# A two-layer decoder on one core: keys and values made further ahead, in room taken from three buffers, with a new hand-written order

## The reference

```python
# layer 0
x = x + self_attn(norm(x))            # 16 heads of 8, causal, softmax
x = x + cross_attn(norm(x), ctx) + bo # 8 heads of 64, keys and values from ctx
x = x + ternary_ffn(norm(x))          # one 128x128 product of quantised values
# layer 1
x = x + self_attn(norm(x))            # scores clipped to +-10, causal
x = x + cross_attn(norm(x), ctx)      # 16 heads of 64
x = x + moe(norm(x))                  # 8 experts of 128x128, gate by softmax,
                                      # gates under 0.1 dropped, rest renormalised
```

## Time and profile before

| | |
|---|---|
| median of 3 runs | 517.37 us (516.3 to 519.82) |
| the profiled execution | 516.53 us, of which the span of the profile is 514.5 us |
| TensorE busy | 491.8 us (96%) |
| TensorE weight loads | 417.4 us (81%) |
| ScalarE busy | 440.0 us (86%) |
| VectorE busy | 409.7 us (80%) |
| POOL busy | 393.6 us (77%) |
| mean granted TensorE clock | 0.991 |

### The profile page before, as it was taken

The page is one execution under the profiler, slowest core; times in us unless marked ns, Lnnn a source line. Parts: engine busy times, 40 slices in busy tenths (PEclk is TensorE's granted clock), DMA queues, the critical chain, the costliest instruction groups (busy, mean ns, idle before and its releaser), DMA issues.

```text
span 514.5 us, 15998 instructions
## 1 busy us (share of the span) xinstructions
PE 491.8 (96%) x5499; PEld 417.4 (81%) x5499; DVE 409.7 (80%) x937; ACT 440.0 (86%) x1177; POOL 393.6 (77%) x557
## 2 busy tenths in 40 slices
PE   7999999999999999999999999999999999989983
PEld 3887886878998888788898888888988888777772
DVE  4868778986898898988888898887888787877663
ACT  5888888999898888998899898999799898798741
POOL 4687588885888788868889776887787787775664
PEclk9999999999999999999999999999999999999996
DMA  6900000000000000000000000000000000000000
GB/s 194 341 5 1 1 3 2 2 2 3 1 2 7 3 8 2 2 6 9 2 1 8 3 5 5 1 6 4 2 11 3 3 2 8 6 2 7 6 6 11
DMA packets 6462, 8.95 MB, mean 17 GB/s; under 512 B 1008, under 2 KB 4848, under 8 KB 6384
## 3 DMA queue, kind: packets, MB, share of 16 engines
q1 hardware_dynamic: 6384, 7.94, 4.7%
HBM read 6.50 MB, written 1.05 MB: 15 GB/s over the span
## 4 chain that ended last, share of the span: by engine, by line
PE 77%; ACT 7%; issue 4%; DVE 4%; POOLq 3%; POOL 3%; DVEq 1%; DMA 0%; ACTq 0%
PE psum L1171 12%; PE psum L1158 9%; PE psum L1198 8%; PE psum L1226 8%; PE psum L1115 8%; PE psum L1145 5%; PE psum L1184 3%; PE psum L1331 2%; PE psum L1237 2%; ACT diff_cross L770 2%; PE psum L1217 2%; PE psum L1186 2%; PE psum L1218 2%; PE psum L1219 2%; PE psum L1209 2%
## 5 line engine op out<-in xcount | busy, mean ns | idle before, releaser
L690 POOL TENSOR_TENSOR w_low_self<-w_self 128x1024 f16<-128x1024 f32 x64 | 120.7, 1894 | 13.9 <-ACT w_self L753 8.6
L770 ACT ACTIVATE diff_cross<-psum,row_max_cross 128x128 f32<-128x128 f32 x384 | 104.5, 410 | 7.9 <-DVE row_max_cross L913 7.4
L695 POOL TENSOR_TENSOR diff_cross<-diff_cross,e_rec_cross 128x1024 f32<-128x1024 f32 x48 | 90.8, 1897 | 14.8 <-DVE e_rec_cross L922 13.9
L913 DVE TENSOR_REDUCE row_max_cross<-psum 128x8 f32<-128x1024 f32 x48 | 58.0, 1218 | 17.8 <-PE psum L1158 17.7
L920 DVE TENSOR_REDUCE e_sum_cross<-diff_cross 128x8 f32<-128x1024 f32 x48 | 58.3, 1215 | 2.0 <-ACT diff_cross L770 1.9
L780 ACT ACTIVATE w_cross<-psum 128x1024 f32<-128x1024 f32 x48 | 49.9, 1049 | 6.0 <-PE psum L1171 5.1
L1158 PE MATMUL psum<-kT_cross,qT_cross 64*128 64x128 f32 x768 | 53.2, 282 | 0.5 <-ACT qT_cross L735 0.3
L1198 PEld LDWEIGHTS psum<-w_cross,v_cross 128*64 128x64 f32 x768 | 41.1, 136 | 15.4 <-issue 13.7
L1198 PE MATMUL psum<-w_cross,v_cross 128*64 128x128 f32 x768 | 51.3, 278 | 0.3 <-issue 0.2
L1158 PEld LDWEIGHTS psum<-kT_cross,qT_cross 64*128 64x128 f32 x768 | 46.0, 187 | 6.4 <-issue 4.2
L1171 PE MATMUL psum<-ident,diff_cross 128*128 128x128 f32 x384 | 49.3, 273 | 0.4 <-ACT by_head_self L735 0.3
(11 more groups left out here) (194 smaller groups left out, 1398.4 us busy)
## 6 DMA issues: line engine op xcount, KB each, us to landing
out_dram<-x_all SPq DMA_DIRECT2D x16, 64.0 KB, 1.5
x_all<-in_x SPq DMA_DIRECT2D x1, 768.0 KB, 7.4
cT_all<-in_ctx SPq DMA_DIRECT2D x1, 768.0 KB, 9.2
e_k<-in_e_k SPq DMA_DIRECT2D x1, 512.0 KB, 4.9
e_v<-in_e_v SPq DMA_DIRECT2D x1, 512.0 KB, 5.8
e_q<-in_e_q SPq DMA_DIRECT2D x1, 512.0 KB, 8.9
e_o<-in_e_o SPq DMA_DIRECT2D x1, 512.0 KB, 9.8
m_w<-in_m_w SPq DMA_DIRECT2D x1, 512.0 KB, 8.7
```

The costliest lines, as they stand in the source:

```text
L690: pool.tensor_tensor(L.w_low[u][:], L.w[u][:], halves(L.w[u][:]), ALU.subtract)\
L695: pool.tensor_tensor(L.diff[u][:].rearrange("p (h k) -> p h k", h=UNIT), L.e[u][:].rearrange("p (h k) -> p h k", h=UNIT), L.e_rec[:, u, :] ...
L770: last = act.activation(L.e[u][:, P * p:P * (p + 1)], S_[:, P * p:P * (p + 1)], ACT.Exp, bias=L.row_max[:, u, p:p + 1])
L913: dve.tensor_reduce(L.row_max[:, u, :], group(i, turn)[:].rearrange("p (h k) -> p h k", h=UNIT), AX_X, ALU.max, negate=True).then_inc(L.ma ...
```

## The change

It does six things.

1. `AHEAD` goes from 6 and 4 to 8 and 6 sequences.
2. The room for that comes from: the cross-attention's `diff` becomes the same buffer as `w` (three buffers less), so the exponentials of a sequence wait until the product with the values of the sequence before is done; `w_low` becomes the unused low 16 bits of each word of `w`, written and read at a step of 4 bytes; the masks are stored once and read four times over by a broadcast operand; `ones` and `mix` move into `weighted`.
3. `weighted` now also holds `mix`, so `ml` of a sequence waits for `o` of the one before.
4. For the last sequence the sum over the experts and the sum with `x` are made by VectorE, not by POOL.
5. `keep_busy` puts 4, 2 and 3 multiplications without use before `xT`, `g` and `e` of the last sequence, into banks that these overwrite.
6. The orders of TensorE, ScalarE, VectorE and POOL are new. The steps are the same ones.

```diff
-AHEAD = dict(cross0=6, cross1=4)
+AHEAD = dict(cross0=8, cross1=6)
...
-            add(f"{L}.ex.{c}", "ACT", 2060, [f"{L}.mx.{c}"], [f"{L}.t.{c}"], half=1030)
+            add(f"{L}.ex.{c}", "ACT", 2060, [f"{L}.mx.{c}"], [f"{L}.pv.{c}"], half=1030)
...
-            self.diff = self.w if width == SD else [sb(f"diff{u}", [P, UN]) for u in range(units)]
+            self.diff = self.w
...
-        self.w_low = [self.sb(f"w_low{u}", [P, UN], FP16) for u in range(2)]
+        self.w_low = [w[:].bitcast(FP16).rearrange("p (n two) -> p n two", two=2)[:, :, 0] for w in self.w]
...
-        mask = [sb(f"mask{j}", [P, 4, P], BF16) for j in range(4)]
+        mask = [sb(f"mask{j}", [P, P], BF16) for j in range(4)]
...
-        mix = sb("mix", [P, P])
+        mix = weighted[:, 1, :]
...
             def mix_experts(i):
+                if i == NSEQ - 1:
+                    return
...
                 act.wait_ge(L.max_ready[u], i + 1)
                 if i:
-                    act.wait_ge(s_full, score(i - 1, f"{L.name}.t.{u}"))
+                    act.wait_ge(x_full, full(i - 1, f"{L.name}.pv.{u}"))
...
                 if i:
-                    dve.wait_ge(mixed, i)
+                    dve.wait_ge(*emptied(i - 1, "moe.b"))
...
             def finish(i):
+                if i == NSEQ - 1:
+                    dve.drain()
+                    dve.tensor_reduce(moe.xn[:], weighted[:].rearrange("p e d -> p d e"), AX_X, ALU.add)
+                    dve.drain()
+                    dve.tensor_tensor(mix, moe.xn[:], x_all[:, i, :], ALU.add)
+                    dve.drain()
+                else:
+                    dve.wait_ge(mixed, i + 1)
                 dve.wait_ge(x_full, full(i, "moe.b"))
-                dve.wait_ge(mixed, i + 1)
...
-                                  ident_b[rows, rows], mask[j][rows, :, :].rearrange("p h k -> p (h k)"),
+                                  ident_b[rows, rows], mask[j][rows, :].unsqueeze(1).broadcast_to([32, 4, P]),
...
+            def keep_busy(place, n):
+
+                for _ in range(n):
+                    pe.matmul(place.rearrange("p (h k) -> p h k", h=4), ident_b[:],
+                              mask[0][:].unsqueeze(1).broadcast_to([P, 4, P]), start=True, stop=True)
...
                 if step == "xT":
+                    room(i, name)
+                    if L is moe and i == NSEQ - 1:
+                        keep_busy(bank(i, name), 4)
                     pe.wait_ge(units_ready if L is ffn else L.xn_ready, i + 1)
```

More of the change, by code:

```diff
@@ L168, in all_steps @@
     add("moe.gTe", "ACT", 167, ["moe.gT"])
-    add("moe.ml", "DVE", 1150, ["moe.e", "moe.w"])
+    add("moe.ml", "DVE", 1150, ["moe.e", "moe.w"], ["moe.o"])
     add("moe.sm", "POOL", 3293, ["moe.ml"], ["moe.o"])
@@ new lines @@
+        "aWb4aSbMbAbPbIbicgbsa8b4cpa3aFbIbPbMaNbAbsaDaFb4cgaScpaWbAcwbibPbMbIa8aNcJcwcpcgb4bsaSaWaFbIbMbPbicJ"
+        "bAa8cwcga3b4cpaNbsaSaFaWbIcJbibMbPa8bAcwcpcga3a3aNaSbsb4aWaFbMbPbIcJbia8aFbAcwcpb4cgbsaNaSaWcJbMbIbi"
+        "bPa8bAaNcwa3cgcpaFb4bsaWaScJbPbibIa3bMa3a8bAcwcgb4aFbIaNbsaScpaWbibPbMcJbAcwa8cpa3aNbscgb4aSaWcJbMbi"
+        "bPa8cwbIbAaNcga3cpaWaSbsb4cJaNbiaSa8a3aWbIbAcwcgcpbMa8bPbsbib4cJbPa3bIcwbibMbsbAcgcpb4cJbsbIbMbPbAcw"
+        "cgcpb4bIbAcJbMbPcwcgbIb4cpbMbPb4cpcgcwcJcgcpcwcJcwcJcJ"
@@ L496, in decoder @@
         x_bias = [sb(f"x_bias{b}", [P, P]) for b in range(2)]
-        ones = sb("ones", [P, P])
         t_abs = sb("t_abs", [P, 1])
@@ L552, in decoder @@
         weighted = sb("weighted", [P, EXPERTS, P])
-        mix = sb("mix", [P, P])
-        t_unit, t_round = weighted[:, 0, :], weighted[:, 1, :]
+        mix = weighted[:, 1, :]
+        t_unit, t_round, ones = weighted[:, 0, :], weighted[:, 1, :], weighted[:, 2, :]
         bias_added = sem("bias_added")
@@ L632, in _ @@
                     for j in range(1, 4):
-                        sp.dma_start(mask[j][32 * j:P, :, :], mask[0][0:P - 32 * j, :, :]).then_inc(masks_turned, 16)
-                        sp.dma_start(mask[j][0:32 * j, :, :], mask[0][P - 32 * j:P, :, :]).then_inc(masks_turned, 16)
+                        sp.dma_start(mask[j][32 * j:P, :], mask[0][0:P - 32 * j, :]).then_inc(masks_turned, 16)
+                        sp.dma_start(mask[j][0:32 * j, :], mask[0][P - 32 * j:P, :]).then_inc(masks_turned, 16)
             for i in range(NSEQ):
@@ L689, in low @@
                     pool.wait_ge(*taken(i, f"{L.name}.s1", u))
-                pool.tensor_tensor(L.w_low[u][:], L.w[u][:], halves(L.w[u][:]), ALU.subtract)\
+                pool.tensor_tensor(L.w_low[u], L.w[u][:], halves(L.w[u][:]), ALU.subtract)\
                     .then_inc(L.low_ready[u], 1)
@@ L709, in mix_experts @@
                 pool.drain()
[L710 removed]
+                pool.tensor_tensor(mix, weighted[:, 0, :], x_all[:, i, :], ALU.add).then_inc(mixed, 1)
             def do_step(i, name, L, step, u):
@@ L776, in weights_by_key @@
                 turn = f"{L.name}.t.{u}"
-                if i:
-                    act.wait_ge(x_full, full(i - 1, f"{L.name}.pv.{u}"))
                 act.wait_ge(s_full, score(i, turn))
@@ L1013, in finish @@
             def finish(i):
+                if i == NSEQ - 1:
[6 more added lines that the diff above has]
+                    dve.wait_ge(mixed, i + 1)
                 dve.wait_ge(x_full, full(i, "moe.b"))
-                dve.wait_ge(mixed, i + 1)
-                dve.tensor_tensor(x_all[:, i, :], bank(i, "moe.b")[:, 0:P], mix[:], ALU.add)\
+                dve.tensor_tensor(x_all[:, i, :], bank(i, "moe.b")[:, 0:P], mix, ALU.add)\
                     .then_inc(emptied(i, "moe.b")[0], 1)
@@ L1092, in _ @@
             dve.memset(shift[:], SHIFT)
-            dve.memset(ones[:], 1.0)
+            dve.memset(ones, 1.0)
             dve.memset(g_weight[:], 0.0).then_inc(consts, 1)
@@ L1129, in self_scores1 @@
                         rows = slice(32 * r, 32 * (r + 1))
-                        pe.matmul(group(i, name, j // 2)[queries, 512 * (j % 2):512 * (j % 2 + 1)],
-                                  ident_b[rows, rows], mask[j][rows, :, :].rearrange("p h k -> p (h k)"),
+                        pe.matmul(group(i, name, j // 2)[queries, 512 * (j % 2):512 * (j % 2 + 1)]
+                                  .rearrange("p (h k) -> p h k", h=4),
+                                  ident_b[rows, rows], mask[j][rows, :].unsqueeze(1).broadcast_to([32, 4, P]),
                                   start=True, stop=False)
@@ L1299, in moe_step @@
                         pe.wait_ge(loaded["moe"], load_count("moe"))
+                    room(i, name)
+                    if i == NSEQ - 1:
+                        keep_busy(bank(i, name), 2)
                     pe.wait_ge(moe_high, i + 1)
-                    room(i, name)
                     pe.matmul(bank(i, name)[:, 0:EXPERTS], moe_xnT[:], wt["m_g"][:], start=True, stop=True)\
@@ L1306, in moe_step @@
                         pe.wait_ge(lo_ready["m_w"], 1)
+                    room(i, name)
+                    if i == NSEQ - 1:
+                        keep_busy(group(i, name)[:, 0:512], 3)
                     pe.wait_ge(*emptied(i, "moe.xT"))
-                    room(i, name)
                     for half in range(2):
@@ L1336, in do_step @@
                     room(i, name)
-                    pe.matmul(bank(i, name)[:, 0:1], ones[:], t_abs[:], start=True, stop=True).then_inc(x_full, 1)
+                    pe.matmul(bank(i, name)[:, 0:1], ones, t_abs[:], start=True, stop=True).then_inc(x_full, 1)
                 elif L in (self0, self1):
```

90 lines of the change are left out of this document (42 added, 48 removed).

## The result

The changed kernel takes 510.61 us (median of four runs, 509.18 to 512.14) against 516.85 us for the kernel before on the same chip (516.3 to 519.82): ratio 0.9867 with an interval of 0.984 to 0.9894, so 1.3% faster (the ratio is of means; the two medians alone give 0.988). The forecast was 512.0 us. The profiled execution spans 507.1 us, against 514.5.

The account below looks back on a forecast made before the run. TensorE, saturated from 130 to 430 us, was taken as the bound, with idle only at the edges. From 516.53 us, 6.8 saved and 2.2 lost give 511.9, stated as 512.0; forecast range 509.5 to 514, chance 0.47.

Parts of the forecast that it names:

- Bound: From 130 to 430 us TensorE idles 0.6 us in 300 and is the bound; added TensorE work costs full price.
- Late fillers: Eight key and value steps moved behind `cross1.y[11]` fill TensorE's waits: 3.6 us saved, bounds 0 and 4.1.
- the two fillers of the last sequence: From 480 us on: cover 1.0 us before `cross1.y[14]` but delay `cross1.t.0[15]`; 0.4 us charged.
- Early fill: Two more key and value steps before `cross1.y[0]` take back 1.0 us of 3.0 idle from 40 to 130 us.
- The tail: Last sequence: `ml` starts 0.4 us earlier, VectorE's sum saves 1.75 us; together 2.2 us, bounds 0.7 and 2.6.
- The start: First scores move ahead of three key steps and wait for masks until some 9.5 us; costs 0.7 us, bounds 0 to 1.3.
- The fallen clock: Rival, chance 0.08: TensorE's longer idle at the start drops its clock; some 4 us of work at half rate, 514 us.
- Changes of shape: Eight more changes of TensorE's array shape, almost all in saturated time, cost 0.14 us each, 1.1 us.
- Buffers: Low halves at a step of 4 bytes and broadcast masks have no price on POOL or TensorE: 0 us.
- the rival with POOL's in-place halves: Rival, chance 0.07: in-place 16-bit writes are dearer on POOL; slower from about 1.4 us more each, 550 us at twice the price.
- The exponentials' wait: ScalarE's new wait for the previous sequence's `pv` is hidden: ahead of the scores in 32 of 45 cases.
- full gain: Rival, chance 0.18: remaining early and late idle vanishes and short gaps in the saturated stretch tighten by 2 us; 507.5 us.

Follow-up runs that it names:

- the run without them: Changed kernel with eight of its eleven key and value steps behind `cross1.y[11]` moved ahead of it: 516.72 us, 0.9988 to the kernel before.
- three swaps: Changed kernel with three late value steps each put behind the step whose wait it covered: 513.13 us in a single run, span 511.1.
- extra products: Changed kernel plus one unused product before each of 64 output projections: with 64 rows (changes array shape) 526.54 us, with 128 rows (control) 515.91 us.
- late scores in this order: Changed kernel with TensorE's first eight and ScalarE's first twelve steps ordered as in the kernel before: 515.49 us, 0.9961 to the kernel before.
- the same two lines: Cross-attention's `diff` placed in `w`, exponentials waiting for `pv`; run with shared halves and masks in the kernel before, old orders and `AHEAD`: 527.99 us, 1.0202.

## Why the prediction was right, point by point

The time lies 1.4 us under the forecast and inside its own range, 509.5 to 514. Several terms were off, in both directions.

**Bound.** Right. The 300 saturated microseconds stayed saturated, and each step put there cost its full time and more (0.80 us for 0.70).

**Late fillers: right in mechanism, too small.** The sum had 3.6 - 0.4 = 3.2 us; idle time gives 4.6, the run without them 5.8. The 3.6 us from 430 to 480 us were near: idle there went from 4.1 us to 0.95. The step that was mis-sized is the 0.4 us charged for the two fillers of the last sequence: in that last stretch (480 to 500 us before, 475 to 494 after) idle went from 2.1 us to 0.63, the 1.0 us before `cross1.y[14]` went and nothing took its place. And a named wait is not all that a cover saves: three swaps cost 2.6 us for 1.8 us of such waits.

**Early fill: right**, 1.5 us by the idle time, 1.0 expected. The two more fillers that stand ahead of `y[0]` are in it.

**The tail: 1.45 us, not 2.2.** (The 1.7 us behind `y[15]` hold 0.3 us more of the store, whose time from the last sum to the end of the span is 1.9 to 2.3 us among these profiles.) The term that was mis-sized is the reduction. It was costed at 1.22 us by L920, which reads neighbours; here the next element to be summed lies 512 bytes further, and 128 sums of 8 are made instead of 8 sums of 128; it took 1.87 us. Which of the two makes the difference, no run sets apart. The start of `ml` was right: 0.35 us earlier relative to the residual sum, 0.4 expected, because the gate weights (500.87) decide now and not the experts (500.27). But the 0.14 us that the dummies bring shows that the clock was little of that.

**The start: the size about right, for another reason.** The sum charged 0.7 us because TensorE would idle longer and "everything that follows is saturated". In the first profile neither shows: idle is 3.6 us against 3.7, the scores began at 9.18 us, 0.3 us sooner than the 9.5 expected, and `cross1.y[0]` is 2.1 us early, 1.5 of it the early fill. But that is the fastest execution. The seven profiles without extra products start `y[0]` at 130.4 to 133.0 us, 132.0 in the middle, against 132.5 before; less the 1.5 us of the early fill, which all but one of them show (idle from 40 to 130 us 1.4 to 1.5 us, in that one 2.0), the start runs from a gain of 0.5 us to a loss of 2.0, with a loss of 1.0 in the middle. That the charge of 0.7 comes near is luck, since the loss is the fallen clock or VectorE behind POOL. And what follows is not TensorE's bound until the first sequence's chain has run: with late scores in this order TensorE waits 4.3 us for VectorE from 13 to 40 us. The prediction looked only at who is idle now, not at what gets late.
The Trainium skill, DMA: Bandwidth & Descriptors (the table at its head), says a transfer under 512 bytes is read, modified and written. The trace doesn't bear out a price here: the last mask copy, with rows of 256 bytes, landed in 1.8 us, with rows of 1024 bytes in 2.2. That is one copy each, and the small one also moves a quarter of the bytes.

**The fallen clock: a rival with too low a chance.** It had 0.08 and came in four of nine profiles of this start, at 1.5 to 2.6 us, about the 2 us forecast. Together with the wait for VectorE it spreads the kernel's times (509.2 to 512.1) rather than decides the verdict.

**Changes of shape: right in kind.** 0.14 us expected, 0.11 measured: 0.9 us for eight, not 1.1. The 0.14 was the difference between two single units and a pair, which can as well be read as the price of two changes, 0.07 each; the measured 0.07 to 0.11 leave both open. TensorEngine Tiling (Array Packing) of the Trainium skill, Key Properties, says that a change drains TensorE, and the trace agrees with these 0.11 us.

**Buffers.** Halves and masks cost nothing (0.9999), as argued from the earlier trace rows; the rival with POOL's in-place halves is out. The exponentials' wait was called hidden; that holds only for the new order. In the old one the same two lines cost 2%. So the new orders avoid a loss of 10 us that no view of the kernel before could show, since the wait didn't exist there.

**The sum by what was measured:** 5.8 (late) + 1.5 (early) + 1.45 (tail) + 0.2 (start) - 0.9 (shape) = 8.05 us, against 7.4 between the profiled spans; with 4.6 for the late fillers it is 6.85. So 7.4 lies between the two readings. It is also the gain of the fastest execution; between the medians it is 6.2 us. The prediction's own sum was 4.6 us. The "full gain" of 507.5 us was not met (510.6 the median; 509.18, the fastest, lies just inside its range). Its reason, shorter gaps inside busy time in the saturated stretch, is not borne out: from `y[0]` to `y[11]` the new order has 6.0 us less of steps by the planner's figures, and takes 4.4 us less.

**What no run separates:** whether `AHEAD` itself was needed, or the places would have sufficed; and what makes TensorE's standstill at the start longer in some executions, with which the clock fell.

## What to carry to other kernels

Work that depends on nothing is worth most where the pipeline runs dry: each such step costs its full time and more while the engine is saturated, and almost nothing between two dependent steps at the end, but only if it stands between exactly those two. A buffer that two stages share is free only in an order that runs the last reader first; look for plain copies queued behind the new wait. In an order written by hand, ask of a moved start which chain it makes late, not only who is idle at that moment.

## What was not expected of the hardware

- A reduction on VectorE over 1024 elements per partition took 1.87 us as 128 sums of elements 512 bytes apart, 1.21 us as 8 sums of neighbours (L920). Three halvings took 0.69, 0.42 and 0.29 us.
- After a warm-up that ended at 6.1 us, TensorE's clock was down from about 9 us on in four of nine profiles whose instructions up to there are the same, and not in the others: the four in which it had stood still longest, 1.69 to 1.93 us against 1.20 to 1.57.
- A VectorE step on 128x128 values in on-chip memory that takes 0.23 us took 1.78 us while POOL worked through 128x1024 products (L1040, without dummies), and ended 0.08 us after POOL's. VectorE's 128x1024 differences from an accumulator (L931) took 1.22 or 1.23 us in the first 40 us of both profiles, also beside a product of POOL.
- Writing 16-bit values at a step of 4 bytes over the operand of the same instruction costs POOL nothing (1900 against 1894 ns), and loading them as weights costs TensorE nothing: L1194 is the load and product of the low halves,

```profile
L1194 PEld LDWEIGHTS psum<-v_self,w_self x512: 96/97/103, 22.9 to 465.3; 128*128 128x128 f16 x171
```

  against 96 ns packed.
